# Two attention layers on one core: layer 0's rough score pieces contract over 64 rows instead of 128

## The reference, cut to what matters

```python
# layer 0: 64 inner channels
theta = theta_w @ xf + theta_b ; phi = phi_w @ xf + phi_b ; g = g_w @ xf + g_b
y = softmax(theta^T phi) @ g^T            # 4096 x 4096 scores per image
x = W_w @ y^T + W_b + xf
# layer 1: 128 inner channels, scores scaled by 128**-0.5
q, k, v = Wq xf + bq, Wk xf + bk, Wv xf + bv
x = x + (softmax(q^T k * scale) @ v)^T
```

## Time and profile before

| | us |
|---|---|
| median of 3 runs | 3435.5 (3430.09 to 3435.86) |
| the profiled execution's own time | 3435.51 |
| its span, first to last instruction | 3433.7 |
| PE busy | 3336.5 (97%) |
| POOL busy | 2965.9 (86%) |
| DVE busy | 2100.6 (61%) |
| ACT busy | 1671.5 (49%) |
| PE weight loads busy | 2113.4 (62%) |
| granted TensorE clock, mean | 0.989 of 2.4 GHz |

### The profile page before, as it was taken

One profiled execution on the slowest core, in us unless ns is written; L12 is line 12 of the kernel. 1 busy time (PEld: TensorE's weight loads), 2 busy tenths in 40 slices (PEclk: granted clock), 3 DMA queues, 4 the chain that ended last, 5 costly groups with the idle time before them and its releaser, 6 DMA issues.

```text
span 3433.7 us, 46684 instructions
## 1 busy us (share of the span) xinstructions
PE 3336.5 (97%) x13124; PEld 2113.4 (62%) x13124; DVE 2100.6 (61%) x3029; ACT 1671.5 (49%) x2241; POOL 2965.9 (86%) x1366
## 2 busy tenths in 40 slices
PE   6999999999999989999999998999999999999998
PEld 4555566666655556666655555666665555566665
DVE  4555576776555557676755555677675555666674
ACT  4455445444455544444445554544454555444444
POOL 4999699898989969898989996989898999688897
PEclk9999999999999999999999999999999999999999
DMA  1000000000000000000000000000000000000000
GB/s 43 13 18 19 28 10 22 12 22 16 19 19 16 19 23 16 16 19 19 13 19 19 19 16 23 19 13 21 16 19 13 19 19 16 19 13 16 13 13 10
DMA packets 34038, 61.73 MB, mean 18 GB/s; under 512 B 5280, under 2 KB 5920, under 8 KB 33568
## 3 DMA queue, kind: packets, MB, share of 16 engines
q1 hardware_dynamic: 33824, 59.23, 5.6%
HBM read 42.44 MB, written 16.78 MB: 17 GB/s over the span
## 4 chain that ended last, share of the span: by engine, by line
PE 91%; DVE 3%; issue 2%; POOL 2%; ACT 1%; SPq 0%; DVEq 0%; DMA 0%; ACTq 0%; POOLq 0%
PE acc_out L471 16%; PE rough L398 15%; PE acc_out L455 13%; PE scores L420 7%; PE scores L423 7%; PE scores L425 7%; PE scores L429 7%; PE scores L426 7%; PE acc_out L443 2%; PE acc_out L441 2%; PE acc_out L442 2%; DVE piece_max L793 2%; PE rough L380 2%; PE acc_out L492 1%; PE acc_out L386 1%
## 5 line engine op out<-in xcount | busy, mean ns | idle before, releaser
L280 POOL TENSOR_TENSOR sums<-sums,probs 128x1024 f32<-128x1024 f32 x886 | 2116.0, 2388 | 145.1 <-ACT probs L718 104.7
L793 DVE TENSOR_REDUCE piece_max<-rough 128x1 f32<-128x512 f32 x2024 | 1309.5, 684 | 649.1 <-PE rough L398 646.2
L810 DVE TENSOR_TENSOR probs<-scores,shift_rows 128x1024 f32<-128x1024 f32 x512 | 626.7, 1224 | 567.3 <-PE scores L429 543.2
L718 ACT ACTIVATE probs<-scores 128x1024 f32<-128x1024 f32 x512 | 520.1, 1025 | 672.8 <-PE scores L423 665.1
L711 ACT ACTIVATE probs<-probs 128x1024 f32<-128x1024 f32 x512 | 539.4, 1053 | 499.6 <-DVE probs L810 499.4
L914 POOL TENSOR_TENSOR p_lo<-probs,p_hi 128x1024 fp32r<-128x1024 f32 x192 | 459.2, 2392 | 188.0 <-ACT probs L711 187.7
L471 PE MATMUL acc_out<-probs,v_vals 128*128 128x512 f32 x1280 | 605.4, 595 | 0.0
L425 PE MATMUL scores<-qry_a,k_hi 128*128 128x512 f32 x1024 | 507.8, 496 | 0.0
L455 PE MATMUL acc_out<-probs,g_vals 128*64 128x512 f32 x2048 | 495.0, 605 | 0.0
L420 PE MATMUL scores<-qry_a,phi_a 128*128 128x512 f32 x1024 | 432.3, 422 | 0.0
L710 ACT ACTIVATE p_hi<-probs 128x1024 fp32r<-128x1024 f32 x192 | 203.3, 1059 | 441.0 <-DVE probs L810 397.2
(11 more groups left out here) (97 smaller groups left out, 2961.0 us busy)
## 6 DMA issues: line engine op xcount, KB each, us to landing
x_q<-x SPq DMA_DIRECT2D x32, 256.0 KB, 2.7
x_res<-x SPq DMA_DIRECT2D x32, 256.0 KB, 3.0
mid<-mid_new SPq DMA_DIRECT2D x32, 256.0 KB, 2.2
x_q<-mid SPq DMA_DIRECT2D x32, 256.0 KB, 2.7
x_res<-mid SPq DMA_DIRECT2D x32, 256.0 KB, 3.2
out<-result SPq DMA_DIRECT2D x32, 256.0 KB, 2.3
x_kv<-x SPq DMA_DIRECT2D x24, 256.0 KB, 2.7
probs<-x SPq DMA_DIRECT2D x2, 1024.0 KB, 6.0
```

The source lines that it names most:

```text
L280: eng.tensor_tensor(sums[:, parity], sums[:, parity], probs[:, s % P_BUFS], ALU.add).then_inc(s_plus, 1)
L793: nc.vector.reduce_max(piece_max[:, t, c:c + 1], src, AX.X).then_inc(s_reduced, 1)
L810: nc.vector.tensor_tensor(probs[:, s % P_BUFS].rearrange("p (h c) -> p h c", c=QB), scores[:, s % 2].rearrange("p (h c) -> p h c", c=QB), ...
```

## The change

Layer 0's rough pieces contract over the 64 rows of hi alone (before, over hi and lo). For even query tiles the piece reads the upper half of the partitions, for odd ones the lower half. For this the keys' hi must be in both halves somewhere: the two halves of `phi_b` and of `qry_b` change places, so that `phi_b` has hi in its upper half and the constant in its lower one, and the shift row goes to the lower half of `qry_b`. Even pieces read `phi_b`, odd ones `phi_a`. The pieces' order, their places in the stream, their banks and their semaphores are as before, as are the pieces of layer 1. POOL waits for its own memset of the constant before it goes on.

```diff
             def rough_piece(layer, parity, piece, place):
                 t, c = piece
-                keys = (phi_a, k_hi)[layer]
-                mm(place, qry_a[:, parity, t * P:(t + 1) * P], cols(keys, c), start=True, stop=True).then_inc(s_rough, 1)
+                at = slice(t * P, (t + 1) * P)
+                if layer == 1:
+                    mm(place, qry_a[:, parity, at], cols(k_hi, c), start=True, stop=True).then_inc(s_rough, 1)
+                elif t % 2 == 0:
+                    mm(place, qry_a[0:IC, parity, at], cols(phi_b, c)[0:IC], start=True, stop=True).then_inc(s_rough, 1)
+                else:
+                    mm(place, qry_a[IC:P, parity, at], cols(phi_a, c)[IC:P], start=True, stop=True).then_inc(s_rough, 1)
...
-                copy(cols(phi_b, c)[IC:P], src[IC:P], PHI_B[IC:P])
+                copy(cols(phi_b, c)[0:IC], src[0:IC], PHI_B[0:IC])
...
-                    copy(qry_b[0:IC, parity], acc_out[0:IC, parity]).then_inc(s_row_sb, 1)
+                    copy(qry_b[IC:P, parity], acc_out[IC:P, parity]).then_inc(s_row_sb, 1)
...
-            nc.gpsimd.memset(phi_b[0:IC, :].bitcast(F32), 1.0 / IC).then_inc(s_ones, 1)
+            nc.gpsimd.memset(phi_b[IC:P, :].bitcast(F32), 1.0 / IC).then_inc(s_ones, 1)
+            pool.wait_ge(s_ones, 1)
```

## The result

The changed kernel takes 3473.2 us (3470.4 to 3474.9, 4 runs) against 3435.0 (3430.1 to 3435.9) before on the same chips: a ratio of 1.0117, 95% interval 1.0104 to 1.0129. It is slower by 36 to 44 us of 3435; the forecast was 3481, slower by 46.

A forecast was written before the change was run, and what follows sets the result against it. PE's instruction stream was taken to bound the blocks. 696 added changes of division at 0.20 us (+139) less 406 pairs at 0.23 (93) gave +46 on 3435.5: 3481 us, range 3400 to 3585.

The forecast's parts named there:

- p: Cost of changing the array's division ahead of a 128-column weight load: 0.09 + 0.11 = 0.20 us, taken from 64-column matmuls.
- The pair at 0.23: Two 64-row pieces on different halves overlap, so a pair takes 0.23 us of array time instead of 0.46.
- The layout at nothing: Swapping the halves of `phi_b` and `qry_b`, with POOL's wait for its memset, costs 0, at most some 0.1 us.
- The terms of the sum: Layer-0 block +1.21 us, x 28 = +34; last layer-1 block +4.0, x 3 = +12; together +46 us.
- pair with undivided work on both sides: Layer-0 pairs at s = 0, 5 and 12: two added changes less the pair's gain, +0.17 us each.
- pair beside a batch: Layer-0 pairs with a value batch on one side: one added change less the pair's gain, -0.03 us each, ten times.
- the single of s = 8: Layer-0 third piece at s = 8 with undivided work on both sides: two added changes, +0.40 us.
- three in a row: Layer-0 third of s = 7 and pair of s = 8; the last waits for DVE, one added change behind, +0.20 us.
- s = 11's third and s = 12's pair together: Layer-0 third piece behind a value batch, +0.20 us, and a pair between undivided work, +0.17 us.
- s = 13's third: Layer-0 single third piece with a value batch before it: one added change, +0.20 us.
- 4 singles x 0.40: Last layer-1 block: four single pieces between undivided work, two added changes each, 0.40 us apiece.
- Rivals 1, 2 and 3: No price, 3342 us (0.12; variant 3404, 0.08); halves don't overlap, 3575 (0.14); 64 rows run undivided, 3435 (0.08).

## Why the prediction was right, point by point

- **Where the time is set.** PE's stream bounds the blocks: right. What is added there is in the block's length, less what a wait takes away; PE busy 63.14 of 63.20 us in the last layer-1 block.
- **p, carried over from 64 columns to 64 rows.** Right, to the hundredth: 0.09 on the way in, 0.09 on the way out, 0.11 for each load that could not be ahead. It was an assumption: the trace before could not show it, nor that two row halves overlap. The Trainium skill's rule (TensorEngine Tiling (Array Packing), section Key Properties) is that changing the mode drains the engine. The trace agrees for rows too, with 0.09 us at each change; the load in the open comes on top.
- **The pair at 0.23.** Right: 0.01 us between the two starts, and 0.23 lost when both use one half.
- **The layout at nothing.** Right within what the times can tell (0.9997); the traces put it at -2.0 us, in the start.
- **The terms of the sum.** Set start against start, the changed layer-0 block and the one before differ by: pair with undivided work on both sides +0.155 to +0.17 (taken: +0.17), pair beside a batch -0.02 to -0.045 (-0.03) but at s = 1, where the second piece waits, +0.03, the single of s = 8 +0.40 (+0.40), three in a row +0.19 (+0.20), s = 11's third and s = 12's pair together +0.35 (+0.37), s = 13's third +0.18 (+0.20).
- **What was mis-sized.** Two terms, both because lateness shortens a wait that was there before; "what stands behind PE is late by the same amount" was taken without that. In the layer-0 block the next queries' projection (s = 14) waits for the last reduction; it takes 0.10 us of the lateness away in the block shown and 0.18 in most others: 1.1 instead of 1.21, 3 us in all. In the last layer-1 block the term "4 singles x 0.40" was too large: a third piece there stands behind a wait already, with its load and the next one's in the open, as these rows of the kernel before show (1.78 us for four instructions at 0.43, and the next start 0.33 behind):

```profile
863.83 1.88 PE L471 MATMUL acc_out<-probs,v_vals 128*128 128x512 f32 x4
865.61 0.50 PE L398 MATMUL rough<-phi_a,qry_a 128*128 128x512 f32 x1
865.94 0.39 PE L425 MATMUL scores<-qry_a,k_hi 128*128 128x512 f32 x1
```

  The four add 0.23, 0.34, 0.23 and 0.05 us, the last because 0.21 us of waiting for DVE was there before. 3.3 per block instead of 4.0, 2 us in all.
- **What was left out.** The blocks that open an image have other neighbours, and gained 6 us together instead of 4 x 1.21. All in all the blocks named gained 42 us where 46 were forecast. The rest of the difference between 46 and 38 us lies outside them: -2.0 in the start, by the layout, and -2.7 in the turns and one late block, which the traces here don't tie to the change.

Rivals 1, 2 and 3 are each excluded by a row above: loads at 286.27 and not ahead, starts 0.01 apart, and 64-row instructions with changed distances.

## What to carry to other kernels

Half the rows for half the work is only worth it where the array is divided already: count the changes of division that a small matmul adds on both its sides, at about 0.2 us each when 128 columns of weights follow, and set against it what runs side by side. Here a pair was worth 0.23 us, so one added change pays and two don't; using the divided form beside the value batches alone beat both kernels (3425.9 us). A change that falls where the engine waits anyway is partly or wholly free, and a batch that looks like pure cost may be what hides another engine's latency.

## What the runs showed of the hardware

A change of the array's division costs the same 0.09 us whether it goes to 64 rows (0.32 instead of 0.23), to 64 columns (0.32) or back (0.42 with the piece's own load of 0.11 in it; 0.52 instead of 0.43 behind a batch), and even between two divided forms (64 rows to 64 columns: 0.43 from the pair's start to the batch, as to undivided scores). In the changed kernel no weights are loaded ahead across it. Two row halves with their own loads start 3 to 6 ns apart in 420 of 421 pairs, though each piece has a semaphore wait of its own. The granted clock stayed at 1.00 in the blocks, in the kernel with both pieces in one half too, where the other half of the rows is idle; the mean of the whole was 0.992 there.
